# Issuing the first row-pair copies behind the direct and layout rows of pairs 0 and 1, with nine warm-up matmuls instead of twelve

## The reference

```python
emb = tables[feat_idx, sparse]                     # (512, 26, 32), a gather of rows
linear_out = lin_sparse_w[feat_idx, sparse].sum(-1) + dense @ lin_dense_w
x0, xk, res = emb, emb, []
for w, bb in ((conv1_w, conv1_b), (conv2_w, conv2_b)):       # w: (128, 676), then (128, 1664)
    hp = einsum('bhd,bmd->bhmd', xk, x0).reshape(-1, h * M, E)   # every row of xk times every row of x0
    xn = sigmoid(einsum('oi,bid->bod', w, hp) + bb)
    xk, keep = xn[:, :64], xn[:, 64:]
    res.append(keep)
cin_out = concat(res).sum(-1) @ cin_w + cin_b
h = concat(emb.reshape(512, 832), dense)
for W, b in ((W1, b1), (W2, b2), (W3, b3)): h = tanh(h @ W + b)  # 1024, 512, 256
return linear_out + cin_out + h @ deep_w + deep_b + bias
```

## Time and profile before

| what | value |
|---|---|
| median of 3 runs | 420.84 us (420.27 to 423.86) |
| the profiled execution | 420.59 us, of it 418.8 us span |
| PE busy | 402.7 us (96%) |
| DVE / ACT / POOL busy | 311.9 / 161.9 / 174.6 us |
| DMA | 73.93 MB, mean 177 GB/s over the span |
| mean granted clock of TensorE | 0.992 of full |

### The profile page before, as it was taken

One profiled execution on the slowest core, in us unless ns is written; L12 is line 12 of the kernel. 1 busy time (PEld: TensorE's weight loads), 2 busy tenths in 40 slices (PEclk: granted clock), 3 DMA queues, 4 the chain that ended last, 5 costly groups with the idle time before them and its releaser, 6 DMA issues.

```text
span 418.8 us, 5255 instructions
## 1 busy us (share of the span) xinstructions
PE 402.7 (96%) x1854; PEld 167.9 (40%) x1854; DVE 311.9 (74%) x347; ACT 161.9 (39%) x269; POOL 174.6 (42%) x146
## 2 busy tenths in 40 slices
PE   3967999999999999999999999999999999999998
PEld 1412233333333333333333333333333335887885
DVE  4104869998989989898989898998989898432223
ACT  3136445435253544544543525354454511112012
POOL 6745473664844754855656600000000255880000
PEclk9979999999999999999999999999999999999999
DMA  5368689999999999999989998899978670430000
GB/s 203 60 142 177 159 185 227 212 237 235 216 230 224 220 236 237 224 235 212 234 227 219 228 226 233 211 221 214 227 189 200 167 186 2 122 79 2 1 0 2
DMA packets 43582, 73.93 MB, mean 177 GB/s; under 512 B 22206, under 2 KB 24638, under 8 KB 43555
## 3 DMA queue, kind: packets, MB, share of 16 engines
q1 hardware_dynamic: 39970, 71.82, 71.5%
q0 software_dynamic: 3584, 1.76, 3.2%
HBM read 71.63 MB, written 1.71 MB: 175 GB/s over the span
## 4 chain that ended last, share of the span: by engine, by line
PE 88%; issue 4%; ACT 2%; another core or an unknown queue 2%; DMA 1%; SPq 1%; DVE 1%; DVEq 0%; ACTq 0%
PE conv L495 43%; PE conv L473 19%; PE conv L516 8%; PE ring L516 7%; PE ring L485 5%; PE ring L455 4%; ACT xk L660 1%; SPq L319 1%; PE ring L531 1%; ACT x L632 1%; DMA idx_sb<-in_idx 0%; ACT res L662 0%; DMA copied<-emb 0%; DVE prod L836 0%
## 5 line engine op out<-in xcount | busy, mean ns | idle before, releaser
L396 POOL DMA_INDIRECT emb<-in_table,rows x112 | 141.9, 1267 | 96.9 <-DMA emb<-in_table,rows 65.2
L836 DVE TENSOR_TENSOR prod<-ring,xk 128x1024 f32<-128x1024 f32 x96 | 114.2, 1216 | 32.3 <-ACT xk L660 27.4
L836 DVE TENSOR_TENSOR copied<-copied,xk 128x1024 f32<-128x1024 f32 x112 | 135.1, 1243 | 0.0
L495 PE MATMUL conv<-copied,w_sb 128*64 128x512 f32 x448 | 105.2, 593 | 0.0
L660 ACT ACTIVATE xk<-conv,const_sb 64x512 f32<-64x512 f32 x64 | 43.7, 683 | 143.1 <-PE conv L473 117.0
L495 PE MATMUL conv<-prod,w_sb 128*64 128x512 f32 x384 | 93.1, 605 | 2.7 <-DVE prod L836 2.7
L473 PE MATMUL conv<-sq,w_sb 117*64 117x512 f32 x384 | 90.7, 608 | 3.4 <-ACT sq L689 3.4
L495 PEld LDWEIGHTS conv<-copied,w_sb 128*64 128x64 f32 x448 | 31.7, 137 | 63.5 <-issue 55.8
L473 PEld LDWEIGHTS conv<-sq,w_sb 117*64 117x64 f32 x384 | 27.7, 139 | 58.8 <-issue 57.7
L405 POOL TENSOR_TENSOR xt_lo<-xt,xt_hi 128x512 fp32r<-128x512 f32 (+1 forms) x7 | 10.9, 1582 | 96.2 <-ACT xt_hi L726 91.6
L649 ACT ACTIVATE sq<-ring 117x512 f32<-117x512 f32 x90 | 48.6, 595 | 3.9 <-issue 3.2
(11 more groups left out here) (99 smaller groups left out, 324.8 us busy)
## 6 DMA issues: line engine op xcount, KB each, us to landing
copied<-laid SPq DMA_DIRECT2D x224, 256.0 KB
wpiece<-in_mlp SPq DMA_DIRECT2D x22, 256.0 KB
raw<-laid SPq DMA_DIRECT2D x56, 52.0 KB
emb<-in_table,rows POOLq DMA_INDIRECT x112, 4.8
laid<-emb SPq DMA_DIRECT2D x16, 96.0 KB
sel_f<-in_sel SPq DMA_DIRECT2D x1, 832.0 KB, 5.6
const_sb<-in_const SPq DMA_DIRECT2D x1, 626.5 KB, 4.1
w_sb<-in_w SPq DMA_DIRECT2D x1, 416.0 KB
```

Source lines behind the costliest of these rows:

```text
L396: pool.indirect_dma_start(out=emb[0:n, i, j, :], out_offset=None, in_=table, in_offset=bass.IndirectOffsetOnAxis(ap=rows[0:n, i, j:j + 1], ...
L495: mm = nc.tensor.matmul(conv[i % 2][c * HALF:(c + 1) * HALF, :], w2_sb[:, t, :], prod_of(r)[:, c, :], start=(t == 0), stop=(t == T2 - 1))
L836: nc.vector.tensor_tensor(prod_of(r)[:, :, :].rearrange("p c n -> p (c n)"), left[:, :, :].rearrange("p c n -> p (c n)"), xk[i % 2][:, :, ...
```

## The change

SP's stream issues copies 0 and 1 no longer between `lay_out(0)` and `direct(1)` but after `lay_out(1)`, ahead of copies 2 to 5. The number of dummy matmuls from the constants goes from 12 to 9, that of the dummies before the sums of pair 1 from 2 to 1. Nothing else differs, and the output is computed the same way.

```diff
-WARM = 12
+WARM = 9
@@ block.sync
             direct(0)
             lay_out(0)
-            for n in range(2):
-                copy(n)
             direct(1)
             lay_out(1)
-            for n in range(2, RC):
+            for n in range(RC):
                 copy(n)
             lay_out(2)
             fetch(2)
@@ block.tensor
             pe.wait_ge(w2_in, 16)
             slot_free("sums", 1, 0)
-            for k in range(2):
+            for k in range(1):
                 nc.tensor.matmul(sums_bank(1, 0)[:, 0, :], w2_sb[:, 0:2, :].rearrange("p t o -> p (t o)"),
                                  w2_sb[:, 0:8, :].rearrange("p t o -> p (t o)"), start=True, stop=True)
```

## The result

The changed kernel takes 425.50 us as the median of 20 runs (423.07 to 427.54). The kernel before, run beside it, takes 422.20 (20 runs). The ratio is 1.0077, 95% interval 1.0055 to 1.0099: slower by 0.8%, where 415.6 us and faster were forecast, and above the range given. The profiled execution has 425.63 us and a span of 423.2, against 420.59 and 418.8 before.

The account below looks back on a forecast made before the run. PE was taken to set the pace, with transfers nearly full (share 0.98). Of a lead of 7.8 to 10.3 us at the start, 5.0 would arrive: 420.59 to 415.6 us, range 411.3 to 420.6.

Parts of the forecast that it names:

- the 2.7 us before the squares: Unexplained gap between sums and squares of pair 0: bounded by 0 and 2.7 us gained, taken as wholly gone.
- The lead of 10.3: DVE's first product moves from 38.81 to 28.5, 10.3 us earlier; 7.8 if the delay before the squares stays.
- (b): Full transfer stretch from 55 on: stream level with the old one, +0.5 taken; 5.0 us of room at copy 18.
- Part 1: Start of PE: three warm-up matmuls fewer let the sums start at 19.1 instead of 21.5, 2.4 us on the path.
- Part 2: SP's first issues: copies 0 and 1 moved, so pair 1's rows land at 25.8, while `fetch(2)` slips 2.4 us.
- How much of the lead arrives: Step from start to end: 5.0 us arrive, 3 to 5 are given back as stalls in pairs 0 to 2.
- (a): Copy 6, tile 12 of pair 0: lands at 54, used at 56.1; with DVE's advance a lead of 4.8 passes.
- Rival 3: Clock falls in pair 0 by idles while tiles 3 and 8 wait for copies: 2.7 to 3.4 us, 418.8; chance 0.05.
- Part 3: One dummy of pair 0 dropped before the sums of pair 1: bounds 0 to 2.7 us lost, taken as 0.
- Rival 4: Slower: copies 0 to 5 delay what pairs 2 and 3 need, so PE waits: 3.3 slower, 423.9; chance 0.09.
- Rival 1: Transfers follow better than forecast, so about 9 us of the start's lead arrive: 411.6 us; chance 0.15.
- rival 2: Transfers follow worse: stream 3 to 3.5 us behind after 55, so about 1.3 arrives: 419.3 us; chance 0.21.

Follow-up runs that it names:

- before_again: The kernel before, unchanged, run again on a chip of the first kind: 417.83 us, ratio 1.0005.
- after: The changed kernel in its first measurement beside the kernel before: 425.50 us, ratio 1.0077.
- after_again: The changed kernel, unchanged, run again on a chip of the first kind: 417.94 us, ratio 1.0009 to the kernel before.
- e11: The kernel before with 9 warm-up matmuls instead of 12, on a chip of the second kind: 419.68 us, ratio 0.9932.
- e2: The kernel before with 9 warm-up matmuls instead of 12, on a chip of the first kind: 417.92 us, ratio 0.9982.
- e1: The kernel before with only the copies moved (12 warm-up matmuls, 2 dummies), on a chip of the first kind: 417.73 us, ratio 0.9976.
- e4: The changed kernel with 5 dummies before the sums of pair 1 instead of 1, first kind of chip: 418.07 us, ratio 0.9972.
- e12: The changed kernel with 5 dummies before the sums of pair 1 instead of 1, second kind of chip: 425.32 us, ratio 1.0055.
- e7: The changed kernel with ACT held by short copies ahead of squares and sigmoids, as its profile shows the gaps: 430.75 us, ratio 1.0225.
- e9: e7 with 5 dummies before the sums of pair 1 instead of 1: 428.35 us, ratio 1.0183.
- e14: e10 with SP's twelve copy issues waiting until ACT has made both halves of xk of chunk 0: 433.19 us, ratio 1.0230.
- e10: The kernel before with only the copies moved (12 warm-up matmuls, 2 dummies), on a chip of the second kind: 426.30 us, ratio 1.0090.
- after_third: The changed kernel as it stands, run a third time, on a chip of the second kind: 425.08 us, ratio 1.0045.
- e3: The kernel before with copies moved and 9 warm-up matmuls, 2 dummies kept, first kind of chip: 417.47 us, ratio 0.9976.

## Why the prediction was wrong

**The step that failed** is "the 2.7 us before the squares": "I take them as gone, since the copies beside which they appear are gone; for the end it turns out not to matter". Both halves were wrong. The gap doesn't come from those copies: it is missing with them (before_again) and 3.7 us long without them (after). What I had bounded by 0 and 2.7 is a late release, which came at several waits of ACT for PE, had no upper bound in one profile, and came in a new place, in front of the first sigmoid. And it did matter, because the sum counted a lead of 7.8 at the worst, where the start came 2.0 us late.

The same step left a term out. The start of 28.5 also lets go, without a word, the second gap of the kernel before: 2.3 us in front of the sigmoid of chunk 1, "remote" in the earlier trace rows, for which DVE's first product waited. The lead of 10.3 is in the main 2.4 (warm-up), 2.7 (first gap), 2.6 (clock) and this 2.3. With both gaps kept the lower bound of the lead was 5.5, not 7.8.

**A second step failed**, in place (b): the rows of pair 3 were to come "about 3 sooner, by the gathers". The layout that needs them was issued at 53.13, against 52.99 before (on one chip of the first kind 53.86 against 54.27). The gathers of pair 2 did start 2.3 sooner, but POOL then waited 7.47 us for their rows instead of 3.67. So the stream wasn't level after 55: copy 8 went at 56.23, not 54.08, there because it also waits for PE to free its buffer. In the measured kernel PE, itself late, never waited for it; on the chip of the first kind it did.

**What held.** Part 1: the warm-up ended at 18.78 and the sums came at 19.66 (19.31 in after_again), forecast 19.1. Alone it is worth 0.7% on a chip of the second kind (e11), 2.9 us against the 2.4 of the sum, and 0.2% on the first (e2). Part 2's working of the start was right where releases come on time, in after_again: squares 19.84 (19.8 forecast), `x_high(1)` 26.08 (25.8), first product 28.81 (28.5), `fetch(2)` 44.4 (43.7), copies 6 at 46.9 (47.4). In the measured kernel the rows of pair 1 were there early as well, but ACT, held at the sigmoid, couldn't use them.

**How much of the lead arrives.** Not tested in the measured kernel, which had none. after_again has DVE's first product 10.0 earlier than the profiled kernel before, and its span is 415.7 against 418.8: 3.1 arrive, forecast 5.0. But this compares two chips. On one chip the lead is 2.3 and none of it shows in the medians. That 3 to 5 us would be given back as waits at copied tiles in pairs 0 to 2 was right in size (4.7), and the place mostly wrong: (a), tile 12 of pair 0, has 0.39 of it and (b), pair 2, 0.84; the rest is at tile 11 of pair 0 and at tile 3 of pair 1, behind the late rows of pairs 2 and 3.

**Rival 3** (clock falls in pair 0) did come, at 0.05, in another form: not from a late copy but from the late sigmoid and `x` of pair 1, behind the one dummy. Its price was some 2.3, forecast 2.7 to 3.4. The form that was forecast came on the first kind of chip, with the old order (before_again) and with the moved copies (e1, e4): there PE waits 3.7, 3.0 and 3.0 us ("under 2 us each") for the product of tile 3 of pair 1, and the granted clock is at its lower level for the 6.8 us from 60 on. **Part 3** was costed at 0 because "the idle there is some 1.6 us"; it was 3.15 and 1.27. Whether the second dummy would have kept the clock is doubtful, since five didn't in e12. The rule of the Trainium skill, "TensorE: Matmul & The Clock Gate", Part 1, by which idle time throttles the array, agrees with these traces: PE idle for 2.95 and 1.42 before tiles of 1.97 (e7), 1.18 and 1.41 before tiles of 1.08 (e9). **Rival 4**, the slower one, named the copies' debt at copy 18; PE doesn't wait there in the measured kernel, and it wasn't the cause: the chance of 0.09 on "slower" came in, but not for its reason. **Rival 1** never had its condition. The sign of **rival 2**, copy 8 later than 54, did come, without the stalls that were to follow from it.

**The account of the loss**: 2.0 us by a later first tile, 2.3 by half clock in pair 0, 4.4 in the span with the rest. It holds for the two profiled executions; the medians differ by 3.3.

**What stays open**: what makes PE's releases late on some chips, and why the order of SP's first issues shifts them. e14 excludes copies in flight beside the gaps. The direct rows of pair 1, issued 3.5 us sooner, and POOL's gathers of pair 2, 2.3 sooner, differ between the orders too; neither was tried alone. Nor is it known whether the recording, whose updates are incomplete on just these chips, has a part. That the moved copies cost through these gaps is what all profiles fit; it wasn't shown by taking the gaps away on the same chip, and most kernels have one profile there.

## What to carry to other kernels

An idle time that no engine's work explains is not evidence about what happens to be in flight beside it: look for the same gap in other places and executions, and give it no credit in a sum. If such gaps exist, order an engine's stream so that work whose input is ready (here `x` of pair 1) doesn't stand behind a wait that may be late, and keep a lead where the order already has one. Time a change of this size on more than one chip: here the same two kernels differ by 0.1, 0.5 and 0.8%. The safe half of the change, nine warm-ups in the old order, was never slower (0.9982, 0.9932, and 0.9909 with the earlier layout). And a transfer that starts sooner doesn't land sooner by as much when it lands beside others: read where the next step waits for it (here POOL, for the rows of pair 2).

## What the runs showed of the hardware

- The same one-core program has two levels by chip, 418 us on two chips and 422 to 423 on two, and the profiles put the difference at the start: on the second kind TensorE's semaphore updates reach ScalarE up to 8.4 us after the matmuls have ended (e10: sums end at 21.57 + 0.96, first square at 30.90), on the first within 0.1 (after_again: `layer1(0,0)` ends at 23.37, sigmoid at 23.47). TensorE's other matmuls go on meanwhile (after: `layer1(0,1)` starts at 32.95, the update for `layer1(0,0)` comes at 35.87), and ScalarE's own updates come within 0.02 of its instructions' ends.
- The late updates come in lumps: in three kernels of different starts (after, e12, after_third) the sigmoid began at 35.95, 35.88 and 35.94, though its matmuls had ended at 31.87, 28.19 and 30.05. In after the updates of the two spread tiles, for which nobody waited yet, are recorded in the same lump, at 35.91 and 35.95, for matmuls that ended at 32.59 and 33.02.
- One stretch at the lower clock in pair 0 costs 2.3 to 2.4 us on the second kind of chip (after, e7 against e9). On the first kind, where the transfers bind, e2 has such a stretch and its median is 0.5 us above that of e3.
